# Who issues the stores of the mixed contexts in the first context attention: GpSimd in place of ScalarE

## The chip, the cores and the metric

One core of a Trainium2 chip. The time is the device time of one execution in microseconds, from runs of the whole program; the median of the runs counts. The program is a block of six parts after each other (context attention, causal attention, experts, a second context attention with film and state space, causal attention, capacity experts). Engines are named as the profile names them: PE (TensorE), ACT (ScalarE), DVE (VectorE), POOL (GpSimd), SP (SyncE).

## The reference

Only the first part matters here. Eight batches of 64 latent rows (width 512, 8 heads of 64) look at a context of 1601 rows of width 384 and at themselves:

```
xn, ln = layernorm(context), layernorm(latents)
q = rmsnorm(ln @ Wq.T) * scale;  k = rmsnorm([xn @ Wk.T, ln @ Wlk.T]);  v = [xn @ Wv.T, ln @ Wlv.T]
x = x + softmax(mask(q @ k.T)) @ v @ Wo.T + bo
```

In the kernel the context part of `probs @ v` is computed as `(probs @ xn) @ Wv.T`: the probabilities first mix the normalised context rows (384 wide), for every batch and head, and the product with Wv comes once, for all batches, at the end of the stage. These mixed rows are what is stored and loaded back.

## The kernel before, in words

The stage is `xattn0` (line 186). It loops over the 8 batches (`b`), and for each over 13 tiles of context rows (`t`) and then over 4 pairs of heads (`p`). `n = 4 * b + p` counts the pairs.

Key phase of a batch (line 721 on ACT, 570 on DVE, 1021 on PE): PE projects a tile of keys (`project`, line 804), DVE adds the bias (`add_bias`, 467), ACT squares it (`square`, 622), DVE sums and normalises, PE transposes the tile (`turn_keys`, 820) and ACT puts it into `k_T`. Between these PE works off the mixing products (`mix_tile`, 878) of the batch before, whose list is `rest`.

Pair phase (line 761 on ACT, 592 on DVE, 1059 on PE): PE makes the scores of a pair, DVE adds the mask and takes the row minimum (`take_scores`, 492, the instruction at line 501), PE swaps the minima of the two halves (`swap_tops`, 852), ACT takes the exponential (641), DVE scales the latent columns (528), PE transposes the probabilities (`turn_probs`, 865) and DVE and ACT copy them out (517 and 650).

After its 13 mixing products a pair's mixed rows go through three steps: `put_mix` (ACT, 652) scales them out of PSUM, `turn_mix` (PE, 892) transposes them, `put_back` (ACT, 660) copies the transposed rows into one of two buffers `mixed_T` and stores the buffer in `mixed_dram`, in three transfers of 64 KB (128 partitions, for two heads 64 numbers each). `put_back` of the first two pairs of a batch comes in the key phase of the next batch (at tiles 1 and 8, lines 731 and 742), that of the third just before the next batch's first exponential (754), that of the fourth in the next batch's pair 1 (767). Of the last batch nothing is stored: it is copied straight into its place (664 to 670).

A semaphore `stored[n % 2]` tells that a buffer is in memory: `put_back` waits for it before it writes that buffer again (672), and SP before it loads the mixed rows back (397). The load-back (399 to 402, 24 transfers) also waits for the last scores and mixes, since it overwrites the keys. `output_heads` (971) and `output_tokens` (999) then use it.

POOL has little in this stage (409 to 440): constants; for each batch, once DVE has taken all scores of the batch before, the mask (431) and the copy of the latent keys into `k_T` (437); after the loop it adds `bo` to x (440), for which DVE waits before the last sum (602). All queues run in the order written here; there is no planner.

Of the kernel before, what the change touches and what calls it, by code (L numbers as in the profile page):

```python
# [16 lines left out]
NB, SEQ, D = 8, 64, 512  # L17
# [4 lines left out]
KC = DC // P  # L22
# [163 lines left out]
def xattn0(g):  # L186
# [5 lines left out]
    PAIRS, SLOTS, HALVES = 4, CT + 1, 2  # L192
# [18 lines left out]
    with Stage(nc, "a") as s:  # L211
# [42 lines left out]
        mixed_T = s.sb("mixed_T", [P, 2, KC, P])  # L254
# [39 lines left out]
        mix_full, mix_out, back_full, back_out = (s.sem("mix_full"), s.sem("mix_out"), s.sem("back_full"),  # L294
                                                  s.sem("back_out"))
        stored = [s.sem(f"stored{i}") for i in range(2)]
# [26 lines left out]
        def mixed_place(k, h):  # L323
            return mixed_places[KC * h + k]
# [83 lines left out]
        @block.gpsimd  # L408
        def _(pool):
            own = Steps(pool, pool_own)  # L410

            pool.memset(mask8[:], 0).then_inc(mask8_made, 1)
            pool.wait_ge(mask8_made, 1)
            pool.memset(mask8[SEQ:P, :, 6 * P:6 * P + SEQ], 1).then_inc(mask8_made, 1)
            pool.wait_ge(mask8_made, 2)
            pool.memset(mean_of, 1.0 / DC).then_inc(made, 1)
            pool.wait_ge(made, 1)
            pool.tensor_copy(swap[:, 0:SEQ], g.ident[:, SEQ:P]).then_inc(made, 1)
            pool.wait_ge(made, 2)
            pool.tensor_copy(swap[:, SEQ:P], g.ident[:, 0:SEQ]).then_inc(made, 1)  # L420
            pool.wait_ge(made, 3)
            pool.tensor_tensor(both[:], swap[:], g.ident[:], ALU.add).then_inc(made, 1)
            pool.wait_ge(made, 4)
            own.did(pool.memset(k_T[:, :, CTX:SLOTS * P], 0.0))
            own.wait()
            for b in range(NB):
                pool.wait_ge(mask_in[b % 2], 32 * (b // 2 + 1))
                if b >= 1:
                    pool.wait_ge(latents_ready, b)
                    pool.wait_ge(scores_out, 2 * PAIRS * b)  # L430
                pool.tensor_scalar(mask[:], mask8[:, b % 2, :], MASKED, -MASKED, ALU.mult, ALU.add).then_inc(mask_ready, 1)  # L431
                pool.wait_ge(mask_ready, b + 1)
                if b >= 1:
                    pool.wait_ge(scores_full, PAIRS * b)
                else:
                    pool.wait_ge(q_out, 2 * NT)
                pool.tensor_copy(k_T[:, :, CT * P:CT * P + SEQ], kl_T[:, :, b * SEQ:(b + 1) * SEQ]
                                 ).then_inc(latents_ready, 1)
            pool.wait_ge(bo_in, 16)
            pool.tensor_tensor(g.x[:], g.x[:], bo[:].unsqueeze(1).to_broadcast([P, NT, D]), ALU.add).then_inc(x_biased, 1)  # L440

# [167 lines left out]
        def _(act):  # L609
# [50 lines left out]
            def put_back(n):  # L660
                b, p = divmod(n, PAIRS)
                act.wait_ge(back_full, n + 1)
                turned_mix = side[:, 0:DC].rearrange("p (k n) -> p k n", k=KC)
                if b == NB - 1:
                    for h in range(2):
                        for k in range(KC):
                            ins = act.activation(mixed_place(k, 2 * p + h)[:, TOK - SEQ:TOK],
                                                 turned_mix[:, k, h * SEQ:(h + 1) * SEQ], ACT.Copy)
                    ins.then_inc(back_out, 1)
                    return  # L670
                if n >= 2:
                    act.wait_ge(stored[n % 2], 16 * KC * (n // 2))
                act.activation(mixed_T[:, n % 2, :, :], turned_mix, ACT.Copy).then_inc(back_out, 1)
                act.wait_ge(back_out, n + 1)
                for k in range(KC):
                    act.dma_start(g.mixed_dram[:, k, 2 * p:2 * p + 2, b * SEQ:(b + 1) * SEQ],
                                  mixed_T[:, n % 2, k, :].rearrange("p (h q) -> p h q", h=2)).then_inc(stored[n % 2], 16)

            def square_heads(n):
                act.wait_ge(proj_full, n + 1)  # L680
# [38 lines left out]
            for b in range(NB):  # L719
                n = PAIRS * b  # L720
                for t in range(CT):
                    if t == 0:
                        root_group(b, 0)
                    if b == 0 and 0 <= t - 3 < 2 * NT:
                        root_heads(t - 3)
                    if b == 0 and 0 <= t - 5 < 2 * NT:
                        put_queries(t - 5)
                    if b == 0 and t == CT - 1:
                        put_v_bias()
                    if t == 1 and b >= 1:  # L730
                        put_back(n - 4)
                    if t == 7 and b >= 1:
                        put_mix(n - 3)
                    square(b, t)
                    if t >= 1 and t in MEASURE_AT:
                        root_group(b, MEASURE_AT[t])
                    if t >= 1:
                        root(b, t - 1)
                    if t >= 3:
                        put_keys(b, t - 3)  # L740
                    if t == 8 and b >= 1:
                        put_back(n - 3)
                    if b == 0 and 0 <= t - 2 < 2 * NT:
                        square_heads(t - 2)
                    for tile in TOKENS_AT.get(t, ()):
                        normalise_tokens(b, tile)
# [6 lines left out]
                if b >= 1:  # L753
                    put_back(n - 2)
# [3126 lines left out]
```

## Time and profile before

| | |
|---|---|
| median of 3 runs | 2274.43 us (2273.58 to 2275.2) |
| profiled execution | 2271.75 us |
| its span, first to last instruction | 2269.6 us |
| granted TensorE clock, mean of the span | 0.971 |
| stores of the mixed rows | 84 issues of 64 KB on ACT's queue, first at 159.8 us |
| the stage of the change | the first 870 us of the span, about |

A row of a timeline gives the start in us, the length in us, engine, line, operation and tiles, the number of instructions merged, and in brackets the idle time of the engine before it and what ended it. Issues of transfers (ACTq, SPq) are shown but not counted as busy: an idle time in brackets includes them. In the groups by line or tile, durations are in ns.

### The profile page before, as it was taken

How to read it: one execution, taken by the hardware profiler on the slowest of the kernel's cores; microseconds unless marked ns; L12 is line 12 of the kernel's file. 1: busy time of each engine (PE TensorE's matmuls, PEld its weight loads, DVE VectorE, ACT ScalarE, POOL GpSimd, SP SyncE). 2: the span in 40 equal slices, each digit the busy share in tenths (PEclk: the TensorE clock that was granted, in tenths of full speed). 3: DMA queues.
4: the chain of work that ended last, by engine and by line, in shares of the span. 5: the costliest groups of instructions: out<-in, count | busy, mean ns of one | idle time of the engine just before them, and what ended most of it. 6: DMA issues, size and time to landing. Idle time of an engine off the chain costs nothing. (4 is left out here: it accounts for less than half of the span.)

```text
span 2269.6 us, 26653 instructions
## 1 busy us (share of the span) xinstructions
PE 2118.3 (93%) x10028; PEld 1259.0 (55%) x10028; DVE 964.6 (42%) x1957; ACT 711.0 (31%) x1417; POOL 481.2 (21%) x527
## 2 busy tenths in 40 slices
PE   7989999999999998899999998888899986899999
PEld 3545555555555543544444443344446644899998
DVE  6555656656556502420000007999932144422120
ACT  2434544545445411321111114445423112111111
POOL 0000000000000001179899713322322001000010
PEclk9999999999999999999999999899999987899999
DMA  6101222221212233378888766443340101675652
GB/s 220 44 20 42 75 74 53 74 84 40 79 44 71 73 94 158 111 290 312 308 311 306 310 223 226 143 159 111 112 167 19 43 10 63 268 264 211 247 215 81
DMA packets 130935, 326.64 MB, mean 144 GB/s; under 512 B 39621, under 2 KB 88805, under 8 KB 111482
## 3 DMA queue, kind: packets, MB, share of 16 engines
q1 hardware_dynamic: 98664, 294.12, 36.1%
q10 hardware_dynamic: 29442, 22.24, 3.1%
q0 software_dynamic: 2704, 8.59, 1.1%
q8 instruction: 82, 1.34, 0.2%
q14 instruction: 43, 0.35, 0.0%
HBM read 302.89 MB, written 20.91 MB: 143 GB/s over the span
## 5 line engine op out<-in xcount | busy, mean ns | idle before, releaser
L887 PE MATMUL a_mix<-a_xn,a_probs_T 128*128 128x384 f32 (+1 forms) x832 | 315.9, 494 | 7.2 <-ACT a_mixed L657 7.2
L816 PE MATMUL a_sc<-a_wk_centred,a_ctx_T 128*128 128x512 f32 x624 | 287.5, 597 | 2.3 <-DVE a_keys L472 2.3
L1959 PE MATMUL c_gate_up<-bc_w_wide,c_h_rows 128*128 128x512 f32 x480 | 210.9, 592 | 0.0
L887 PEld LDWEIGHTS a_mix<-a_xn,a_probs_T 128*128 128x128 f32 (+1 forms) x832 | 144.9, 191 | 106.2 <-issue 62.9
L816 PEld LDWEIGHTS a_sc<-a_wk_centred,a_ctx_T 128*128 128x128 f32 x624 | 117.5, 191 | 125.5 <-issue 104.5
L1863 DVE TENSOR_TENSOR c_hidden<-c_silu,c_gate_up 128x512 f32<-128x512 f32 x38 | 26.1, 688 | 359.6 <-PE c_gate_up L1959 359.6
L1959 PEld LDWEIGHTS c_gate_up<-bc_w_wide,c_h_rows 128*128 128x128 f32 x480 | 90.1, 190 | 108.1 <-issue 108.1
L2414 PE MATMUL f_ring<-f_picked_T,f_w 128*128 128x160 f32 x1024 | 143.5, 300 | 0.0
L2429 PE MATMUL f_ring<-f_hidden,f_w 128*128 128x160 f32 x1024 | 141.4, 300 | 0.4 <-ACT f_hidden L2304 0.4
L2414 PEld LDWEIGHTS f_ring<-f_picked_T,f_w 128*128 128x128 f32 x1024 | 139.9, 190 | 0.2
L2429 PEld LDWEIGHTS f_ring<-f_hidden,f_w 128*128 128x128 f32 x1024 | 139.3, 190 | 0.9 <-ACT f_hidden L2304 0.6
L431 POOL TENSOR_SCALAR a_mask<-a_mask 128x896 bf16<-128x896 uint8 x8 | 7.5, 940 | 612.3 <-DVE a_top L501 593.0
L2002 PE MATMUL c_y<-c_w_down,c_hidden_T 128*128 128x512 f32 x304 | 136.6, 592 | 0.0
L472 DVE SCALAR_TENSOR_TENSOR a_keys<-a_k_bias,a_std,a_sc 128x512 f32<-128x512 f32 (+1 forms) x104 | 77.0, 741 | 129.2 <-PE a_sc L816 129.2
L627 ACT ACTIVATE a_sq<-a_keys 128x512 f32<-128x512 f32 (+1 forms) x104 | 65.5, 630 | 183.6 <-DVE a_keys L472 183.0
L501 DVE CUSTOM_DVE_ANT_0 a_probs<-a_sc,a_mask 128x896 f32<-128x896 f32 x64 | 67.3, 1089 | 83.3 <-PE a_sc L847 83.3
L2873 DVE MAX8 d_best<-d_left 128x8 f32<-128x1601 f32 x48 | 87.6, 1826 | 1.4
L2877 DVE MATCH_REPLACE8 d_left<-d_best,d_left 128x1601 f32<-128x1601 f32 x48 | 86.9, 1811 | 0.0
L2002 PEld LDWEIGHTS c_y<-c_w_down,c_hidden_T 128*128 128x128 f32 x304 | 54.9, 190 | 55.0 <-issue 55.0
L488 DVE SCALAR_TENSOR_TENSOR a_keys<-a_length,a_most,a_keys 128x512 f32<-128x512 f32 (+1 forms) x104 | 78.2, 751 | 3.6
L3089 PE MATMUL d_ks<-cd_context_T,cd_wk 128*128 128x512 f32 (+1 forms) x192 | 71.0, 525 | 8.4 <-DMA cd_context_T<-in_ctx_T 6.6
L2541 POOL TENSOR_TENSOR c_ss_tmp<-c_ss_tmp 128x2048 f32<-128x2048 f32 (+5 forms) x48 | 76.8, 1601 | 3.8
(560 smaller groups left out, 3260.3 us busy)
## 6 DMA issues: line engine op xcount, KB each, us to landing
bc_w_wide<-in_L_ffn_W SPq DMA_DIRECT2D x64, 1024.0 KB, 5.5
f_w<-in_L_ffn_W SPq DMA_DIRECT2D x32, 2048.0 KB, 8.7
c_w_down<-in_L_ffn_W SPq DMA_DIRECT2D x34, 1024.0 KB, 7.2
a_ctx_T<-in_ctx_T SPq DMA_DIRECT2D x48, 384.0 KB, 3.5
a_xn<-in_ctx SPq DMA_DIRECT2D x24, 768.0 KB, 7.8
d_context<-in_ctx SPq DMA_DIRECT2D x8, 2304.0 KB
cd_context_T<-in_ctx_T SPq DMA_DIRECT2D x21, 768.0 KB, 11.5
mixed_context<-a_mixed_T ACTq DMA_DIRECT2D x84, 64.0 KB, 1.8
```

Of the source, the lines that this page charges most:

```text
L472: dve.scalar_tensor_tensor(out=keys[0:m, n % 4, :], in0=k_bias[0:m, :], scalar=std[0:m, t:t + 1], in1=key_bank(b, t)[0:m, :], op0=ALU.mult ...
L488: dve.scalar_tensor_tensor(out=heads, in0=inverse.unsqueeze(2).to_broadcast([m, 8, 64]), scalar=most[0:m, t:t + 1], in1=heads, op0=ALU.min ...
L816: last = pe.matmul(key_bank(b, t), ctx_T[:, n % AHEAD, k, cols], wk_centred[:, k, :], start=(k == 0), stop=(k == KC - 1))
L887: ins = pe.matmul(mix[:, 0:DC], probs_T[0:m, t, p * P:(p + 1) * P], xn[0:m, b % 2, t, :], start=(t == 0), stop=(t == CT - 1))
L1959: last = pe.matmul(gate_up[2 * (u % 2) + part][:], h[:, k, :], w_wide[:, i % WIDE_RING, k, :], start=(k == 0), stop=(k == KD - 1))
L2002: last = pe.matmul(y[t % 2][:], hidden_T[:, u % 2, k, :], w_down[:, i % DOWN_RING, k, :], start=(c == 0 and k == 0), stop=(c == 1 and k == ...
L2414: last = pe.matmul(ring[use % 3][:, (m - lo) * CAP:(m - lo + 1) * CAP], w1[:, i % CHUNKS, k, at:at + P], picked_T[:, e % 2, k, :], start=( ...
L2429: last = pe.matmul(ring[use % 3][:, (m - lo) * CAP:(m - lo + 1) * CAP], w2[:, i % CHUNKS, k, at:at + P], hidden[:, k, :], start=(k == 0), ...
L2541: own.did(pool.tensor_tensor(out, a, b, op))
L2873: own.did(dve.max(eight, src))
L2877: ins = dve.match_replace(left[:, r, :], eight, src, MASKED)
L3089: last = pe.matmul(bank_of_keys(b, c)[:, 0:hi - lo], wk[:, k, :], context_T[:, k, lo:hi], start=(k == 0), stop=(k == KC - 1))
```

## The change

ACT's `put_back` keeps its wait for the buffer and its copy; its wait for the copy's end and its three `dma_start` are taken out. POOL gets a helper `store(b, p)` that waits for `back_out` (ACT's copies, counted) and issues the same three transfers with the same semaphore. It calls it for the four pairs of batch b - 1 after the mask and the latent keys of batch b, so for batches 0 to 6, as before. PE, DVE and SP are not changed.

```diff
--- before.py
+++ after.py
@@ -423,6 +423,14 @@
             pool.wait_ge(made, 4)
             own.did(pool.memset(k_T[:, :, CTX:SLOTS * P], 0.0))
             own.wait()
+
+            def store(b, p):
+                n = PAIRS * b + p
+                pool.wait_ge(back_out, n + 1)
+                for k in range(KC):
+                    pool.dma_start(g.mixed_dram[:, k, 2 * p:2 * p + 2, b * SEQ:(b + 1) * SEQ],
+                                   mixed_T[:, n % 2, k, :].rearrange("p (h q) -> p h q", h=2)).then_inc(stored[n % 2], 16)
+
             for b in range(NB):
                 pool.wait_ge(mask_in[b % 2], 32 * (b // 2 + 1))
                 if b >= 1:
@@ -436,6 +444,9 @@
                     pool.wait_ge(q_out, 2 * NT)
                 pool.tensor_copy(k_T[:, :, CT * P:CT * P + SEQ], kl_T[:, :, b * SEQ:(b + 1) * SEQ]
                                  ).then_inc(latents_ready, 1)
+                if b >= 1:
+                    for p in range(PAIRS):
+                        store(b - 1, p)
             pool.wait_ge(bo_in, 16)
             pool.tensor_tensor(g.x[:], g.x[:], bo[:].unsqueeze(1).to_broadcast([P, NT, D]), ALU.add).then_inc(x_biased, 1)
 
@@ -671,10 +682,6 @@
                 if n >= 2:
                     act.wait_ge(stored[n % 2], 16 * KC * (n // 2))
                 act.activation(mixed_T[:, n % 2, :, :], turned_mix, ACT.Copy).then_inc(back_out, 1)
-                act.wait_ge(back_out, n + 1)
-                for k in range(KC):
-                    act.dma_start(g.mixed_dram[:, k, 2 * p:2 * p + 2, b * SEQ:(b + 1) * SEQ],
-                                  mixed_T[:, n % 2, k, :].rearrange("p (h q) -> p h q", h=2)).then_inc(stored[n % 2], 16)
 
             def square_heads(n):
                 act.wait_ge(proj_full, n + 1)
```

## Rows read from the trace of the kernel before

**Rows 1.** The page, part 1: busy us, share of the span, instructions.

```profile
PE 2118.3 (93%) x10028; PEld 1259.0 (55%) x10028; DVE 964.6 (42%) x1957; ACT 711.0 (31%) x1417; POOL 481.2 (21%) x527
```

**Rows 2.** Windows 300 to 700 us: length, then busy us (count) by engine.

```profile
sum 400.00, PE 393.30 PEld 216.70 DVE 231.08 ACT 189.24 POOL 6.69; mean PE 98.32 PEld 54.18 DVE 57.77 ACT 47.31 POOL 1.67
```

**Rows 3.** Timeline of POOL: start, us, engine, line, operation [idle before].

```profile
421.38 0.94 POOL L431 TENSOR_SCALAR a_mask<-a_mask 128x896 bf16<-128x896 uint8 x1 [90.83 <-DVE a_top L501]
...
698.15 0.94 POOL L431 TENSOR_SCALAR a_mask<-a_mask 128x896 bf16<-128x896 uint8 x1 [90.83 <-DVE a_top L501]
...
765.45 4.53 POOL L440 TENSOR_TENSOR x<-x,a_k_bias 128x2048 f32<-128x2048 f32 x1 [65.90 <-DMA a_k_bias<-in_L_xattn_bo]
```

**Rows 4.** Timeline of PE, one batch.

```profile
460.27 0.88 PE L887 MATMUL a_mix<-a_xn,a_probs_T 128*128 128x384 f32 x2 [0.32 <-ACT a_mixed L657]
...
483.61 0.66 PE L828 MATMUL a_turned<-ident,a_keys 128*128 128x128 f32 x4 [0.60 <-DVE a_keys L488]
```

**Rows 5.** The tile a_mixed_T: durations min/median/max, and landing.

```profile
L676 ACTq DMA_DIRECT2D mixed_context<-a_mixed_T x84: 360/491/1590, 159.8 to 782.6; - x84
...
DMA to landing us min/median/max: 1.6/1.8/6.7
```

**Rows 6.** Timeline of ACT around the four kinds of stores.

```profile
398.00 1.41 ACTq L676 DMA_DIRECT2D mixed_context<-a_mixed_T  x3
...
402.95 1.04 ACT L641 ACTIVATE a_probs<-a_probs,a_shared_top 128x896 f32<-128x896 f32 x1 [2.22 <-DVE a_shared_top L509]
...
412.70 1.44 ACTq L676 DMA_DIRECT2D mixed_context<-a_mixed_T  x3
...
415.81 0.60 ACT L650 ACTIVATE a_probs_T<-a_turned 128x512 f32<-128x512 f32 x1 [3.14 <-PE a_turned L875]
...
436.61 1.40 ACTq L676 DMA_DIRECT2D mixed_context<-a_mixed_T  x3
...
438.46 0.63 ACT L627 ACTIVATE a_sq<-a_keys 128x512 f32<-128x512 f32 x1 [1.89 <-DVE a_keys L472]
...
742.94 2.51 ACTq L676 DMA_DIRECT2D mixed_context<-a_mixed_T  x3
...
745.87 0.63 ACT L627 ACTIVATE a_sq<-a_keys 128x512 f32<-128x512 f32 x1 [2.96 <-DVE a_keys L472]
```

**Rows 7.** Line 1760, POOL's indirect stores.

```profile
L1760 POOL DMA_INDIRECT dispatched<-hn,c_slot x8: 972/972/1220, 971.9 to 981.1; - x8
...
DMA to landing us min/median/max: 2.7/2.7/3.0
```

**Rows 8.** Timelines of SyncE's queue and of PE, end of the stage.

```profile
788.08 7.22 SPq L401 DMA_DIRECT2D a_k_T<-mixed_context  x14
...
804.75 1.20 SPq L405 DMA_DIRECT2D a_keys<-latent_probs  x2
...
816.80 2.79 PE L983 MATMUL a_sc<-a_k_T,a_wk_centred 128*64 128x512 f32 x12
...
819.52 1.43 PE L991 MATMUL a_sc<-a_keys,a_latent_v 64*64 64x64 f32 x32
```

**Rows 9.** Timelines of DVE and PE, head pairs 0 and 1 of a batch.

```profile
399.92 1.09 DVE L501 CUSTOM_DVE_ANT_0 a_probs<-a_sc,a_mask 128x896 f32<-128x896 f32 x1 [6.31 <-PE a_sc L847]
...
400.94 1.09 DVE L501 CUSTOM_DVE_ANT_0 a_probs<-a_sc,a_mask 128x896 f32<-128x896 f32 x1
...
402.37 0.28 PE L855 MATMUL a_side<-a_top,a_swap 128*128 128x2 f32 x2
...
416.17 0.26 DVE L528 TENSOR_SCALAR a_probs<-a_probs,a_latent_share 64x64 f32<-64x64 f32 x1
...
416.48 0.88 PE L875 MATMUL a_turned<-ident,a_probs 128*128 128x128 f32 x6
```

**Rows 10.** Timelines of POOL and DVE at an indirect store.

```profile
974.76 0.97 POOL L1760 DMA_INDIRECT dispatched<-hn,c_slot  x1 [0.30 <-issue]
...
974.95 0.28 DVE L1841 TENSOR_TENSOR c_equal<-c_place,c_slot_f 128x32 f32<-128x32 f32 x2
```

## The prediction

> **What bounds the kernel now.** I read the page first: its engine line has TensorE (PE) busy for 93% of the span and the other engines' own work (DVE, ACT, POOL) under half [rows 1]. The change lies in the first 800 us, so the next view is the windows from 300 to 700 us, four hundred microseconds inside the loop over the batches. There PE is busy for 393.3 of 400 us, ScalarE (ACT) for 189.2, VectorE (DVE) for 231.1, GpSimd (POOL) for 6.7 [rows 2]. So PE sets the pace of this stage, and whatever the change gives to ACT counts only where PE waits for ACT. The third view is PE's timeline of one batch, for exactly those waits. A batch takes 92.26 us (POOL's mask, once a batch, stands at 421.38 and three batches on at 698.15 [rows 3]) and has three gaps worth the name: two of 0.32 us that end with `mixed` from ACT (one of them is shown) and one of 0.60 us that ends with a key tile from DVE [rows 4]. The 0.32 us before 460.27 is what `put_mix` costs between two uses of one PSUM tile: ACT itself had waited for PE there. No store stands ahead of it.
>
> **Part 1: what ACT is rid of.** 84 issues of 491 ns median [rows 5] are 84 x 0.491 = 41 us, with 28 waits of ACT for its own copy. They stand in 28 groups of three, four kinds of place per batch, and I read in ACT's timeline what ended the idle time behind each kind [rows 6]:
> - head pair 2: issues 398.00 to 399.41, then the table load, then the exponential that waits 2.22 us for DVE. Slack 2.2 us.
> - pair 3: issues end at 414.14, the next copy waits for PE until 415.81. Slack 1.7 us.
> - pair 0 (key tile 1 of the next batch): issues end at 438.01, the next square waits for DVE until 438.46. Slack 0.45 us.
> - pair 1 (key tile 8): at its worst the three issues take 2.51 us and end at 745.45; the next square starts at 745.87, again released by DVE. Slack 0.42 us.
> The idle time printed there holds the issues, since issuing isn't counted as busy; so the slack is start minus end of the issues. All are positive: ACT never comes late because of a store. What this part is worth: 0. Cover of the zero: DVE and PE, which release ACT later than the stores let it go. Were that cover gone, the 41 us would count in full. The bound on the gain is the PE gaps that name ACT, 2 x 0.32 x 7 = 4.5 us, and I take 0 of it, since ACT stood waiting for PE just before them.
>
> **Part 2: what POOL gets.** 84 issues, and no row shows a plain load or store issued by POOL. The nearest is POOL's indirect store of `hn` into `dispatched`, 128 rows: 0.97 us an issue, landing 2.7 us after it, at most 3.0 [rows 7]; between two of them the trace leaves 0.3 us. Lower end of the price: ACT's 0.49 us. Upper end: a store here is cut into 128 x 2 = 256 runs of 256 B, twice as many as the 128 rows, so 1.94 us. I take 0.97, by the row of the same engine and direction. Three issues are then 3 x 0.97 + 2 x 0.3 = 3.5 us, at the upper end 6.4 us. POOL is busy 1.3 us in a batch of 92 us, so four groups of 3.5 or even 6.4 us fit.
>
> What is queued behind them on POOL, and who waits:
> - The mask and the latent keys of the next batch. They wait for DVE's last scores and start at 421.38 [rows 3]. The last group before them starts when ACT's copy is done, about 412.70, and ends at 416.2, at the upper end at 419.1: 5.2 or 2.3 us early. And DVE takes the first scores with the new mask only one batch after 399.92, at 492.2, 70 us later.
> - The bias add on x (765.45, 4.53 us [rows 3]) now comes behind the last group: 781.7 + 3.5 = 785.2 (781.7 is 412.70 and four batches), done at about 790. DVE needs x only after the output projection, whose first product is at 816.80 [rows 8]. Cost 0.
> - The two `mixed_T` buffers: `put_back(n)` waits for store n-2. The shortest distance is pair 2 to pair 0, 398.00 to 436.61 less the copy, some 38 us, against 3.5 + 3.0 (upper: 6.4 + 6.7, the worst landing of rows 5). Cost 0.
> - The end of the stage: SyncE loads the mixed contexts back after the last store. It starts at 788.08, on PE's last scores, not on the store. The last store would land at 781.7 + 2 x 1.27 + 2.7 = 786.9; that is 1.1 us early. With the upper prices (issue starts 781.7 + 2 x 2.24 = 786.2, landing 6.7) 792.9, so the loads start 4.8 us late. PE uses the first of them at 816.80 and the latent rows, issued at 804.75, at 819.52 [rows 8]; 4.8 us off 14.8 us still leaves ten. Cost 0 in both.
>
> **Part 3: does POOL's issuing get in DVE's way?** Two groups fall where PE waits closely on DVE. Pair 2: issues from 398.0 to about 401.5, while DVE reduces scores from 399.92 to 402.03 and PE's swap of the tops starts at 402.37, 0.34 us of slack. Pair 3: issues from 412.7 to 416.2, while DVE scales the latent columns at 416.17 and PE turns them at 416.48 [rows 9]. The trace has one place of the same kind: at 974.76 an indirect issue of POOL runs 0.97 us, and two DVE products of 32 columns with both inputs in SBUF start 0.19 us into it, take 0.28 us together and have no wait before them [rows 10]. So by the rows the price is 0. The upper end is that a DVE instruction stands until POOL's issue is over: pair 2, DVE would want 399.92 and the second issue runs 399.27 to 400.24, 0.3 us, then up to a whole third issue of 0.97, less 0.34 slack: 0.9 us; pair 3, 416.2 - 416.17, nothing to 0.1. Some 1.0 us a batch, 7 us in seven batches.
>
> A rule speaks against the change. The Trainium skill, "SBUF — State Buffer", section "Who interferes with whom", says that VectorE and GpSimd share one pair of SBUF ports under an exclusive lock, so that the second to come is blocked for the whole instruction, and that descriptors made by GpSimd wait behind a VectorE instruction in a two-port mode. By it the stores would be held up by at most the DVE instruction under way, which moves landings inside the slack above and leaves the sum as it is; DVE held up by the issues would be the 7 us. The rows at 974.76 don't agree with the second.
>
> **Sum.** 0 (ACT) + 0 (POOL) + 0 (DVE). The profiled execution took 2271.75 us, its span 2269.6; the median of the three runs is 2274.43, 2.7 above. I forecast the median unchanged: **2274.4 us**. A difference of 0.2%, 4.5 us, is about what a measurement of this kernel can tell.
>
> **Rivals.**
> - *DVE is held up by POOL's issues* (slower): 7 us, 2281.5 us. For it: both groups lie within half a microsecond of PE's waits. Against it: the row at 974.95. It decides from 0.65 us a batch on (4.5 / 7). Chance 0.08, with 0.01 more for POOL's issues so long (over 12 us a group) that `put_back` or the last loads wait for them.
> - *PE's gaps behind ACT close* (faster): 4.5 us at the very most, 2269.9 us. It would need ACT to be the late one in `put_mix`; it waits for PE there. With it goes that some issue of ACT is on a path that the idle times hide. Chance 0.05.
> - *The change does not take work off ACT*: a wait of ACT for `stored` takes the place of the issues, since a buffer comes free later. It would have to exceed 38 us less the group; ACT's timeline would show the wait before L673. Time the same, 2274.4. Chance 0.01.
> - *No effect*, the forecast: 0.85.
>
> **The numbers.** Time 2274.4, the likeliest case. The range goes up by part of the DVE rival, 5 us (two thirds of its price, since the overlaps need not all be full), and down by 3 us, two thirds of the ACT gaps: 2271.4 to 2279.4. Left out are about 0.05 above and 0.03 below. Faster by over 0.2%: 0.05. Slower: 0.09. Same: 0.86, the last two cases together.
>
> **What would show it.** Right: the batch still takes 92.26 us on PE, the gaps of 0.32 and 0.60 us stand where they were, the squares and exponentials of ACT start at the same places after a longer idle time, with the same releasers; POOL has 84 issues of 0.9 to 2 us; DVE's score reduction stays at 1.09 us with PE's swap 0.34 us behind. Wrong: a new gap of PE before the swap of the tops or before the latent transposes of pair 1, a wait of ACT before L673, or the first load of the mixed contexts moved far past 788 with PE idle at 816. If PE's busy share in 300 to 700 us rises from 98.3%, the gain that I put at 0 was there.

## The result and the profile after

The changed kernel takes 2280.86 us in the median of 8 runs (2277.88 to 2286.0), against 2274.81 us in the median of 8 runs of the kernel before (2273.26 to 2275.98). The ratio is 1.0027, 95% interval 1.0019 to 1.0036: 6.1 us, 0.27%, slower. I had forecast 2274.4 us and a range of 2271.4 to 2279.4.

The move itself did what was foreseen. The first view is the tile a_mixed_T in the changed kernel (durations in ns, min/median/max):

```profile
L431 POOL DMA_DIRECT2D mixed_context<-a_mixed_T x84: 707/721/957, 161.5 to 785.0; - x84
...
DMA to landing us min/median/max: 2.0/2.0/5.8
```

84 issues on GpSimd, 0.72 us each, landing 2.0 us after; I had taken 0.97 and 2.7. ScalarE's 41 us of issuing [rows 5] are gone, and nothing of it shows in the stage: the windows of the changed kernel, as in [rows 2], have TensorE (PE) as busy as before.

```profile
sum 400.00, PE 392.84 PEld 216.25 DVE 231.60 ACT 189.79 POOL 44.41; mean PE 98.21 PEld 54.06 DVE 57.90 ACT 47.45 POOL 11.10
```

392.8 of 400 us where it was 393.3. The batch still takes 92.26 us and PE's gaps are those of [rows 4]; in the changed kernel's timeline of PE:

```profile
461.66 0.88 PE L894 MATMUL a_mix<-a_xn,a_probs_T 128*128 128x384 f32 x2 [0.32 <-ACT a_mixed L668]
...
485.00 0.66 PE L835 MATMUL a_turned<-ident,a_keys 128*128 128x128 f32 x4 [0.60 <-DVE a_keys L499]
```

So seven batches are as they were. Inside the stage the loss has one place. The timelines of GpSimd (POOL), VectorE (DVE) and PE in pair 1 of the last batch, changed kernel:

```profile
783.56 2.13 POOL L431 DMA_DIRECT2D mixed_context<-a_mixed_T  x3 [12.56 <-ACT a_mixed_T L684]
785.70 4.53 POOL L451 TENSOR_TENSOR x<-x,a_k_bias 128x2048 f32<-128x2048 f32 x1
```

```profile
786.56 0.15 DVE L535 RECIPROCAL a_share<-a_side 64x1 f32<-64x1 f32 x1
786.75 3.53 DVE L539 TENSOR_SCALAR a_probs<-a_probs,a_latent_share 64x64 f32<-64x64 f32 x1
790.21 0.25 DVE L539 TENSOR_SCALAR a_probs<-a_probs,a_share 64x64 f32<-64x64 f32 x1
```

```profile
780.24 1.73 PE L854 MATMUL a_sc<-a_k_T,a_q_T 64*64 64x448 f32 x16
...
786.20 0.81 PE L894 MATMUL a_mix<-a_xn,a_probs_T 128*128 128x384 f32 x2
790.34 1.54 PE L882 MATMUL a_turned<-ident,a_probs 128*128 128x128 f32 x6 [3.33 <-DVE a_probs L539]
791.81 3.26 PE L854 MATMUL a_sc<-a_k_T,a_q_T 64*64 64x448 f32 x16
```

The addition of `bo` to x, 4.53 us, stood at 765.45 before [rows 3]; now it comes behind the last store, from 785.70 to 790.23. DVE's scaling of 64 latent columns, 0.26 us in [rows 9], starts at 786.75 and takes 3.53 us: it ends when the addition does. PE, which transposes these columns next, has a gap of 3.33 us that wasn't there.

And one thing more follows. The windows of the changed kernel across that place (length, then busy us and counts of PE, PEld, DVE, ACT and POOL, then clock, DMA share and GB/s):

```profile
785.00:789.00 4.00, 2.01 (x15) 1.32 (x13) 3.41 (x6) 1.62 (x3) 3.99 (x2) 1.00 0.12 34
789.00:796.00 7.00, 5.66 (x24) 2.63 (x25) 2.87 (x4) 1.51 (x3) 1.22 (x1) 0.51 0.00 0
796.00:865.00 69.00, 63.93 (x341) 34.15 (x341) 6.57 (x22) 12.28 (x40) 0.00 (x0) 1.00 0.31 98
```

PE's granted clock is 0.51 of full speed from 789 to 796, its lower level of 1.2 GHz, after four microseconds in which PE was busy for 2.0. The row of PE at 791.81 shows what that costs: 16 score products take 3.26 us instead of the 1.73 us of the pair before (at 780.24). Measured at the same PE instruction in the two traces, the changed kernel is 1.6 us late at 780 (1.4 of it since 140, before which the clock had been lower in other places), 7.5 us late at 790, that is 5.9 more, and 5.8 us late at 870, since the kernel before has a stretch of low clock of its own at 801 which the changed one lacks. The windows of the kernel before:

```profile
800.00:810.00 10.00, 9.62 (x27) 5.79 (x28) 0.03 (x1) 1.04 (x7) 0.00 (x0) 0.83 1.00 309
```

The profiled run of the changed kernel is one of the two longest of its eight (2285.91 us, span 2283.9 us). The rest of its lateness comes after the stage: 2.7 us between 865 and 1000, 3.3 us between 1400 and 1500, 2.9 us after 1900. The first experiment below has 2.6 and 3.8 us at the first two places without the stall, so they aren't the stall's. They aren't the stores' either: a kernel below with the stores on ScalarE ("the same instruction 1.4 us later") has 2.4 us at the first, and one with the stores on GpSimd ("the addition after the last pair") has 0.3 at the second.

### The profile page after: what moved, and what is told of

Read it like the earlier page. It is cut to its first block and busy times, and to the rows that moved or that the text cites. A ratio compares the mean times of both kernels' runs of the same rounds, so it can differ in the third digit from the quotient of the medians.

```text
span 2283.9 us, 26653 instructions
## 1 busy us (share of the span) xinstructions
PE 2126.8 (93%) x10028; PEld 1263.6 (55%) x10028; DVE 968.2 (42%) x1957; ACT 711.5 (31%) x1417; POOL 541.7 (24%) x611
## 5 line engine op out<-in xcount | busy, mean ns | idle before, releaser
L431 POOL DMA_DIRECT2D mixed_context<-a_mixed_T x84 | 60.4, 724 | 531.8 <-ACT a_mixed_T L684 516.2
L2810 POOL TENSOR_TENSOR d_scores<-d_scores,d_left 128x1601 f32<-128x1601 f32 x15 | 51.0, 3401 | 121.1 <-ACTq L2963 121.0
```

## Experiments

Theory 1: the addition of `bo`, pushed behind the last store, shuts DVE's scaling out until it ends; PE waits 3.3 us, and the low clock behind the gap costs some more. The stores on GpSimd cost nothing. Rival: the stores themselves cost the time.

Each time stands beside runs of the kernel before made together with it. The ratio and its 95% interval are as recorded; the ratio isn't the quotient of the two medians, from which it differs by up to 0.0009. The medians of the kernel before are 2274.91 us beside the first three experiments and the held store, 2275.68 beside the pieces and the first two runs with seven instructions, 2275.95 beside the two forms tried once, and 2273.95 beside these forms tried seven times and the memset. Diffs are shortened, with `...` for what is left out.

**The addition back to its place** (stores still on GpSimd):

```diff
                     for p in range(PAIRS):
+                        if b == NB - 1 and p == 2:
+                            pool.wait_ge(bo_in, 16)
+                            pool.tensor_tensor(g.x[:], g.x[:], bo[:]..., ALU.add).then_inc(x_biased, 1)
                         store(b - 1, p)
-            pool.wait_ge(bo_in, 16)
-            pool.tensor_tensor(g.x[:], g.x[:], bo[:]..., ALU.add).then_inc(x_biased, 1)
```

> The changed kernel, with GpSimd's addition of bo to x put between the stores of pairs 1 and 2 of batch 6, about where it ran before the change. Theory 1 (the addition, moved behind the last store, shuts VectorE's scaling of the latent columns out until it ends, 3.3 us of TensorE, and the half clock that follows costs some 3 more; the stores on GpSimd cost nothing): the 3.53 us instruction is 0.25 us again, TensorE's gap of 3.33 us is gone, time 2274.8 us, within 1.5 us of the kernel before. Rival (the 84 issues on GpSimd cost the time themselves): 2280 us, as the changed kernel.

2273.34 us (11 runs, 2269.16 to 2276.8), ratio 0.9991, 0.9982 to 0.9999. The scalings are 0.25 us throughout and the gap is gone. Beside these runs the kernel before has 2274.91 us and scatters more, from 2270.61 to 2279.58. The 6 us are gone although all 84 issues are on GpSimd: the rival falls. At 0.09% with the interval ending at 0.9999 I don't call it a gain.

**The addition late, stores on ScalarE** (the kernel before, with one wait more):

```diff
+            pool.wait_ge(totalled, PAIRS * (NB - 1) + 2)
             pool.wait_ge(bo_in, 16)
             pool.tensor_tensor(g.x[:], ...)
```

> The kernel before, stores on ScalarE, with one more wait: GpSimd adds bo to x only after TensorE's totals of pair 1 of the last batch, 784.3 us in the profile of before, so that the addition lies over VectorE's scaling at 785.2. Theory 1: a scaling of about 3.7 us, a gap of TensorE as long, a low clock after it, 2281 us. Rival (the stores on GpSimd are the cause): no change, 2274.8 us.

2280.01 us (8 runs), ratio 1.0025, 1.0015 to 1.0035: the whole loss, with none of the change's stores. PE's timeline has the gap:

```profile
787.63 1.05 PE L876 MATMUL a_turned<-ident,a_probs 128*128 128x128 f32 x6 [3.56 <-DVE a_probs L529]
```

**The addition after the last pair**:

```diff
+            pool.wait_ge(latents_scaled, 2 * PAIRS * NB)
             pool.wait_ge(bo_in, 16)
```

> The changed kernel, with the addition of bo held until VectorE has scaled the last latent columns of the stage (about 798 us). Theory 1: nothing of the pair phase lies under the addition any more; VectorE's three scalings of wv, 1.28 us, may wait up to 4.5 us for it but TensorE needs them 18 us later; 2274.8 us. Rival (the stores): 2280 us.

2272.86 us (12 runs), ratio 0.9997, 0.9988 to 1.0006. The same shutting out happens, where it costs nothing: the three scalings of wv (line 601 in the kernel before) take 4.6 us together instead of 1.3, and PE doesn't need them yet. DVE's timeline:

```profile
797.08 4.61 DVE L613 TENSOR_SCALAR a_wk_centred<-a_wk_centred,a_gain 128x512 f32<-128x512 f32 x3
```

**The addition in four pieces**:

```diff
-            pool.tensor_tensor(g.x[:], g.x[:], bo[:]..., ALU.add).then_inc(x_biased, 1)
+            for t in range(NT):
+                pool.tensor_tensor(g.x[:, t, :], g.x[:, t, :], bo[:], ALU.add).then_inc(x_biased, 1)
...
-            dve.wait_ge(x_biased, 1)
+            dve.wait_ge(x_biased, NT)
```

> The changed kernel, with the addition of bo cut into four instructions, one for each 512 columns (about 1.15 us each), at the same place behind the last store. Theory 1 with a lock held for one instruction: VectorE's scaling waits for the piece under way only, at most 1.1 us, so TensorE's gap falls from 3.3 us to at most 1.1, perhaps once more for the second scaling; 2275 to 2277 us. If the lock is kept while GpSimd has work queued: gap 3.3 us and 2280 us as in the changed kernel.

2275.17 us (11 runs), ratio 0.9998, 0.9989 to 1.0007. The pieces take 1.28 us each. Timelines of DVE and PE in it:

```profile
783.82 0.30 DVE L540 TENSOR_SCALAR a_probs<-a_probs,a_latent_share 64x64 f32<-64x64 f32 x1
784.03 1.31 DVE L540 TENSOR_SCALAR a_probs<-a_probs,a_share 64x64 f32<-64x64 f32 x1
```

```profile
785.40 0.55 PE L883 MATMUL a_turned<-ident,a_probs 128*128 128x128 f32 x3 [0.68 <-DVE a_probs L540]
```

The first scaling slipped in where one piece ended, the second waited for the next piece, and PE for 0.68 us. What shuts DVE out is one instruction, not GpSimd being busy.

**Seven times over.** To have the effect above the scatter I gave the kernel before (stores on ScalarE) a GpSimd instruction of 3.6 us in each of batches 1 to 7, started when PE has the totals of pair 1. It adds zero to x in place, so x keeps its values.

```diff
                                  ).then_inc(latents_ready, 1)
+                if b >= 1:
+                    pool.wait_ge(totalled, PAIRS * b + 2)
+                    own.did(pool.tensor_tensor(g.x[:], g.x[:], g.zero[:].to_broadcast([P, NT, D]), ALU.add))
+                    own.wait()
```

> The kernel before (stores on ScalarE), with an instruction of GpSimd added in batches 1 to 7 (x plus zero, in place, 128x2048, 4.5 us, the value of x unchanged), started after the totals of pair 1, so over VectorE's scaling of the latent columns. Theory 1: seven gaps of 3.7 us of TensorE, 26 us, and with the half clock behind each (another 3 us, as after the one gap of the changed kernel) 26 to 50 us: 2301 to 2325 us. Rival (GpSimd's work beside VectorE costs nothing): 2274.8 us.

2304.94 us (4 runs) against 2275.68, ratio 1.012, 1.0102 to 1.0137: 29 us in the medians. Each scaling under it takes 2.85 us and PE waits for 2.65:

```profile
425.14 2.85 DVE L532 TENSOR_SCALAR a_probs<-a_probs,a_latent_share 64x64 f32<-64x64 f32 x1
```

```profile
333.20 0.88 PE L879 MATMUL a_turned<-ident,a_probs 128*128 128x128 f32 x6 [2.65 <-DVE a_probs L532]
...
428.05 1.54 PE L879 MATMUL a_turned<-ident,a_probs 128*128 128x128 f32 x6 [2.65 <-DVE a_probs L532]
```

The starts of the seven instructions measure what each costs, since the batch is 92.26 us without them. POOL's timeline:

```profile
233.23 3.60 POOL L441 TENSOR_TENSOR x<-x,zero 128x2048 f32<-128x2048 f32 x1 [84.83 <-PE a_side L865]
...
329.50 3.60 POOL L441 TENSOR_TENSOR x<-x,zero 128x2048 f32<-128x2048 f32 x1 [84.83 <-PE a_side L865]
...
424.34 3.60 POOL L441 TENSOR_TENSOR x<-x,zero 128x2048 f32<-128x2048 f32 x1 [84.83 <-PE a_side L865]
...
520.70 3.60 POOL L441 TENSOR_TENSOR x<-x,zero 128x2048 f32<-128x2048 f32 x1 [84.90 <-PE a_side L865]
```

233.23 to 329.50 is 96.27 us, 4.0 more than a batch; 329.50 to 424.34 is 94.84, 2.6 more; then 4.1 again. Alternately the gap alone and the gap with 1.4 us on top. The windows behind the first four gaps tell why:

```profile
236.00:240.00 4.00, 3.06 (x18) 1.74 (x22) 1.61 (x3) 1.48 (x3) 0.83 (x1) 0.57 0.07 15
331.00:335.00 4.00, 1.79 (x18) 1.16 (x22) 2.88 (x3) 1.44 (x4) 2.10 (x1) 1.00 0.41 108
427.00:431.00 4.00, 2.95 (x14) 1.70 (x18) 1.72 (x3) 1.37 (x3) 0.94 (x1) 0.59 0.09 22
522.00:526.00 4.00, 1.59 (x14) 1.00 (x18) 3.08 (x3) 1.44 (x4) 2.30 (x1) 1.00 0.44 122
```

After the first and third the granted clock is at its lower level for most of the window, after the second and fourth it is full. What decides between them I can't say from these runs; all four had the same gap of 2.65 us before them. The fifth and the seventh gap are followed by the lower clock too, the sixth isn't. At the same PE instructions the seven cost 24.0 us together; 2.8 more come between 870 and 1000, where the first experiment has 2.6 without any gap.

**The same instruction 1.4 us later**, after the scaling of pair 1 (`pool.wait_ge(latents_scaled, 2 * (PAIRS * b + 2))` in place of the wait for `totalled`):

> The same seven instructions, started 1.4 us later, once VectorE has scaled the latent columns of pair 1: they lie over PSUM copies, the score reduction with one input in SBUF and nothing of the scaling form, and end before the next scaling. Theory 1 (only the form with both ends in SBUF is shut out): no gap, 2274.8 us, at most 2 us more. Rival (any VectorE instruction beside a GpSimd addition is slowed): the 1.09 us reductions and 0.56 us copies longer, 2280 us and more.

2277.7 us (10 runs), ratio 1.0008, 0.9998 to 1.0018. GpSimd has the same 25 us more to do, and 27 of the 29 us are gone. The copies out of PSUM (0.56 us) and the score reductions (1.09 us) under it keep their usual length. One overlap is left: in the last batch the addition of `bo` follows at once and reaches the scaling of pair 2, which takes 1.41 us for 0.25; the copy of 0.69 us before that scaling keeps its length. So what counts is which DVE instruction lies under GpSimd's.

**Do the stores shut DVE out too?** As the first experiment, with the store of pair 3 held so that its issues lie over the scaling in the seven batches that have stores on the way:

```diff
+                        if p == 3:
+                            pool.wait_ge(totalled, PAIRS * b + 2)
                         store(b - 1, p)
```

> As a_add_early (addition early), and GpSimd's store of pair 3 held until TensorE's totals of pair 1 are there, so that its three issues lie over VectorE's scaling of the latent columns in all seven batches. If an issue on GpSimd shuts VectorE out as the addition does (0.71 us each): 0.1 to 0.7 us a batch, the scaling up to 0.9 us long, TensorE with a gap before the transposes, up to 5 us in all, 2279 us. If only GpSimd's computing instructions do: scaling 0.25 us, no gap, 2274.8 us. I expect the second.

2273.2 us (11 runs), ratio 0.9998, 0.999 to 1.0007. POOL's and DVE's timelines:

```profile
413.35 2.14 POOL L431 DMA_DIRECT2D mixed_context<-a_mixed_T  x3 [15.17 <-PE a_side L872]
```

```profile
413.93 0.26 DVE L543 TENSOR_SCALAR a_probs<-a_probs,a_latent_share 64x64 f32<-64x64 f32 x1
414.10 0.26 DVE L543 TENSOR_SCALAR a_probs<-a_probs,a_share 64x64 f32<-64x64 f32 x1
```

Three issues from 413.35 to 415.49, two scalings under them, 0.26 us each. They don't. In the same trace the third issue of pair 2 (397.44 to 398.18) lies over the score reduction that starts at 397.68, which takes its usual 1.09 us. This is what part 3 of the prediction had asked, and its answer, 0, was right.

**Which form of DVE's instruction?** Two variants of the changed kernel, addition late as it is:

```diff
-                    dve.tensor_scalar(latents, latents, scale, None, ALU.mult)
+                    dve.tensor_scalar(latents, latents, scale, 0.0, ALU.mult, ALU.add, accum_out=unused[...])
```

```diff
-                    dve.tensor_scalar(latents, latents, scale, None, ALU.mult)
+                    dve.tensor_tensor(latents, latents, scale.to_broadcast([SEQ, SEQ]), ALU.mult)
```

> The changed kernel, addition late as it is, but VectorE scales the latent columns with the form that also writes an accumulator (into two spare columns). If only the plain scaling form, SBUF to SBUF, is shut out by the addition: 0.25 to 0.35 us each plus the accumulator's read, no gap of 3.3 us, and time 2275 us plus some tenths of a us a pair where the longer chain shows (29 pairs, up to 5 us). If any VectorE instruction with SBUF at both ends is shut out: 3.5 us once more and 2280 us or above.

> The changed kernel, but VectorE scales the latent columns by a product of two operands in SBUF (columns times the factor, broadcast). If a second input in SBUF is shut out while GpSimd reads SBUF: the first product under the addition takes 3.4 us or so, gap 3.3 us, time 2280 us. If only the scaling form is: no gap, 2275 us.

The traces are clear. DVE's timelines, of the one and of the other:

```profile
787.13 0.28 DVE L540 TENSOR_SCALAR_CACHE_REDUCE a_probs<-a_probs,a_latent_share 64x64 f32<-64x64 f32 x1
...
787.34 0.28 DVE L540 TENSOR_SCALAR_CACHE_REDUCE a_probs<-a_probs,a_share 64x64 f32<-64x64 f32 x1
```

```profile
782.79 3.57 DVE L539 TENSOR_TENSOR a_probs<-a_probs,a_latent_share 64x64 f32<-64x64 f32 x1
786.28 0.22 DVE L539 TENSOR_TENSOR a_probs<-a_probs,a_share 64x64 f32<-64x64 f32 x1
```

The form with an accumulator runs in 0.28 us right under the addition (786.08 to 790.65), with no gap of PE; the product of two operands in SBUF is shut out until it ends (786.26). The times are not: 2277.88 us (1.0003, 0.9993 to 1.0014) and 2276.22 us (1.0007, 0.9997 to 1.0018) against 2275.95 us. The intervals overlap, and the second is below the 2280 us that I had expected of a kernel with this gap. One place in a run is too little against such a scatter, so both forms went under the seven instructions of 3.6 us:

> e_dose_on (seven additions of 3.6 us over VectorE's scaling) with the scaling in the form that also writes an accumulator. If that form isn't shut out, as one instance in h_accum showed: no gap of 2.65 us, 2276 us where e_dose_on took 2305. If it was luck of a few tenths there: 2300 us and more.

> e_dose_on with the scaling as a product of two operands in SBUF. If it is shut out like the plain form, as in i_two_inputs: seven gaps of 2.7 us, delays of 2.6 us or, with a stretch of half clock behind, 4.0 us each, together 24 to 28 us: 2300 to 2305 us. If the time of i_two_inputs (2276 us) meant that this form costs less: 2285 us or below.

2278.67 us (11 runs; 1.0014, 1.0005 to 1.0023) and 2304.33 us (4 runs; 1.0134, 1.0119 to 1.015), against 2273.95. The product is shut out as the plain scaling is. The seven gaps of the product are 2.68 us each and cost 2.5 to 5.4 us: here six of the seven are followed by the lower clock. The accumulator form isn't shut out: the gaps are gone. It is 4.7 us slower than the kernel before in the medians, of which the trace has 0.55 us inside the batches (from 140 to 780 us, at the same PE instructions) and no gap. Another 2.5 come between 870 and 1000, where the first experiment has as much without this form; for the remainder no cause is shown.

**Does it need an instruction that reads SBUF?** The kernel before, with a memset of hT (dead by then) over the scaling, batches 1 to 7:

```diff
+                    pool.wait_ge(totalled, PAIRS * b + 2)
+                    own.did(pool.memset(g.hT[:], 0.0))
+                    own.wait()
```

> The kernel before, stores on ScalarE, with a memset by GpSimd (hT, 128x2048, dead by then; it only writes, about 1.8 us) over VectorE's scaling in batches 1 to 7. If an instruction that only writes shuts the scaling out too: the first scaling about 1.1 us long in seven batches, gaps of about 0.8 us, 5 to 7 us in all, 2281 us. If only one that reads SBUF does: 0.25 us, no gap, 2275 us.

2279.62 us (11 runs), ratio 1.0027, 1.0018 to 1.0036. POOL's and DVE's timelines:

```profile
417.40 1.80 POOL L441 MEMSET hT<- 128x2048 f32 x1 [84.80 <-PE a_side L865]
```

```profile
418.22 1.03 DVE L532 TENSOR_SCALAR a_probs<-a_probs,a_latent_share 64x64 f32<-64x64 f32 x1
418.39 0.90 DVE L532 TENSOR_SCALAR a_probs<-a_probs,a_share 64x64 f32<-64x64 f32 x1
```

Both scalings end at 419.25 to 419.29, just after the memset's end at 419.20. An instruction that only writes shuts the plain scaling out as well, for 0.78 us of PE's time a batch, and behind none of these seven short waits does the clock fall. Whether a memset shuts out the product of two operands too wasn't run.

## Why the prediction was wrong

- **Where it failed**: in part 2, the point on the bias add. I wrote that the addition "now comes behind the last group: 781.7 + 3.5 = 785.2, done at about 790. DVE needs x only after the output projection [...]. Cost 0." The time was right (785.70 to 790.23, in a trace 1.6 us late by then). The cost was not: the addition cost a gap of PE of 3.33 us and, with the low clock behind it, 5.9 us at that place. The step asked only who waits for its result, not what runs beside it. DVE's scaling of pair 1 in that batch stood at 416.17 + 4 x 92.26 = 785.2, a number I had in [rows 9], and the addition is a GpSimd instruction six times as long as an issue. I had looked for a DVE instruction under a GpSimd one in part 3, but only under the issues that were added, not under the instruction that was moved. The sign that I had named, a new gap of PE before the latent transposes of pair 1, came true, in one batch and by the addition.
- **The row that I missed**: the trace of the kernel before has the same thing later in the program. Its timelines of POOL and of DVE:

```profile
1637.72 3.02 POOL L2803 TENSOR_TENSOR d_scores<-d_scores,d_left 128x1601 f32<-128x1601 f32 x1 [12.66 <-ACTq L2956]
```

```profile
1637.87 2.93 DVE L2901 TENSOR_SCALAR d_share<-d_quarter,d_total 128x64 f32<-128x64 f32 x1
```

  A scaling of 64 columns from SBUF to SBUF starts 0.15 us into a computing GpSimd instruction and takes 2.93 us, to that one's end; the other execution of the same line takes 0.35 us. I had taken the place at 974.76, an issue, as the one of its kind. For an instruction that computes, this row gives the price.
- **The rival**: "DVE is held up by POOL's issues", 0.08, had the right engine pair and the right instruction of pair 1, and the wrong GpSimd instruction. Its price, 7 us in seven batches, is near the measured 6.1 us by chance: the issues cost 0 (the held store shows it), and one addition cost 3.3 us plus the clock.
- **The rule of the Trainium skill** ("SBUF — State Buffer", "Who interferes with whom") that I weighed was the right one, set against the wrong instruction. The prediction told it without its conditions. The section names VectorE forms that can be shut out, among them `tensor_scalar`, except the form that writes out its accumulator, and an instruction with two inputs in SBUF, the latter only against a GpSimd instruction that reads SBUF. The runs agree in each case tried: the plain scaling (3.53 us for 0.26) and the product of two operands in SBUF (3.57 for 0.22) are shut out by the addition; the form that writes its accumulator isn't (0.28); and the memset shuts out the plain one (1.03). My row at 974.95 [rows 10] spoke only of an issue, and for an issue it was right.
- **The size**: the gap of 3.33 us is direct, and the low clock behind it is the rest at that place. Three traces have one such gap. At the same PE instructions the changed kernel loses 5.9 us there, the kernel with the addition late and the stores on ScalarE 5.1 us (gap 3.56), the one with the product of two operands 5.0 us (gap 3.37), and the granted clock is low behind each. The windows of the last:

```profile
787.00:791.00 4.00, 4.00 (x21) 1.37 (x20) 1.33 (x2) 1.51 (x3) 0.00 (x0) 0.57 0.00 0
```

  The kernel before loses 1.7 us a little later, at 801, which the first and the third of them don't; so by 870 the three have lost 4.2, 5.1 and 3.3 us against it. The average over runs stays open: the kernel with the product has a ratio of 1.0007 (up to 1.0018, 4.1 us), where the changed kernel's interval begins at 1.0019. The changed kernel itself was measured in 8 runs and not beside the variants, and no kernel was run that has the gap and keeps the clock.
- **Right**: ACT's issues were worth 0 in the stage; the mask, the buffers and the load-back had room; POOL's issues are cheap (0.72 us, even below the 0.97 taken). The late addition also explains the load-back starting at 795.14 rather than 788.08: it follows PE's last scores.
- **The range**: up to 2279.4 by "two thirds of the price" of one rival. It missed by 1.5 us. With the addition's overlap priced at its length, up to 4.5 us and once, it would have been a case of its own.

## What to carry to other kernels

When work is put into an engine's queue, what stands behind it moves too. Each instruction that moves needs two questions: who waits for its result, and what will now run beside it; a GpSimd instruction of several microseconds must not land on a plain VectorE scaling from SBUF to SBUF, or on a VectorE product of two operands in SBUF, that TensorE is waiting for. The form that also writes an accumulator wasn't held up in any run here. Here the stores could move for nothing, if the addition stayed ahead of the last two of them or went behind the last pair.

## What the runs showed that I had not expected

- A 0.25 us instruction of VectorE took 3.5 us beside one GpSimd addition, and 2.85 beside a 3.6 us one, each time to its end; a GpSimd memset does the same, GpSimd's own DMA issues do not.
- The same scaling with an accumulator output takes 0.28 us instead of 0.25 and wasn't shut out once: both scalings under each of the seven additions kept their 0.28 us.
- Of seven gaps of 2.65 us in a stream of TensorE work at full clock, four were followed by the lower clock, for 1.4 us more each; in another kernel with seven gaps of 2.68 us, six were. The single gaps of 3.3 to 3.6 us were followed by it in all three traces.
- The kernel before scattered from 2273.26 to 2275.98 us in its first 8 runs, from 2270.61 to 2279.58 in 32 later ones, and up to 2282.98 in another 21. Differences of 3 us need more than the trace of one run on each side.
